# The rotary step of an attention block: pair swaps by a VectorE shuffle instead of swapped projections, and q one slot earlier

## The reference, cut to what matters

```python
x = x + attn(layernorm(x), W_attn, W_proj)       # 16 heads of 8, causal softmax
x = x + ffn(layernorm(x), gate_w, experts)       # 8 experts, Sinkhorn gates, top 64 tokens each

q, k, v = split(x @ W_attn)
q = q * cos + rotate_half(q) * sin               # rotate_half: (x1, x2) -> (-x2, x1) on each pair
k = k * cos + rotate_half(k) * sin
att = softmax(where(causal, q @ k.T / sqrt(8), -inf)); y = att @ v; out = y @ W_proj
```

## Time and profile before

| | us |
|---|---|
| median of 3 runs | 493.18 (491.93 to 494.08) |
| profiled execution, its own time | 492.21 |
| its span, first to last instruction | 490.5 |
| TensorE busy (mean granted clock 0.962 of full) | 418.8 (85%) |
| VectorE busy | 404.0 (82%) |
| ScalarE busy | 308.9 (63%) |
| GpSimd busy | 228.1 (47%) |

### The profile page before, as it was taken

The page is one execution under the profiler, slowest core; times in us unless marked ns, Lnnn a source line. Parts: engine busy times, 40 slices in busy tenths (PEclk is TensorE's granted clock), DMA queues, the critical chain, the costliest instruction groups (busy, mean ns, idle before and its releaser), DMA issues.

```text
span 490.5 us, 9349 instructions
## 1 busy us (share of the span) xinstructions
PE 418.8 (85%) x2827; PEld 209.1 (43%) x2827; DVE 404.0 (82%) x1616; ACT 308.9 (63%) x599; POOL 228.1 (47%) x411
## 2 busy tenths in 40 slices
PE   5448987998999999899999989999988965999563
PEld 4233444464545546344554644555444432434121
DVE  6968756898898789788878978887986876996997
ACT  1002684788678769867876986887777432543871
POOL 3142573567466356746635674543433210000895
PEclk9955988999999999999999999999999999999998
DMA  8770143035027004402701440270001010100122
GB/s 261 213 174 2 49 135 76 34 115 113 21 78 182 25 33 131 99 20 77 182 25 45 126 110 2 97 162 24 2 1 64 2 43 0 43 23 21 43 65 86
DMA packets 28434, 36.85 MB, mean 75 GB/s; under 512 B 2144, under 2 KB 24224, under 8 KB 26912
## 3 DMA queue, kind: packets, MB, share of 16 engines
q1 hardware_dynamic: 27312, 34.68, 25.4%
q10 hardware_dynamic: 1072, 1.57, 1.3%
HBM read 19.41 MB, written 16.78 MB: 74 GB/s over the span
## 4 chain that ended last, share of the span: by engine, by line
PE 53%; DVE 23%; ACT 8%; issue 7%; DMA 5%; POOL 1%; SPq 1%; POOLq 1%; DVEq 1%; ACTq 0%
PE PVB L494 11%; PE ROWB L469 10%; PE CHB L482 9%; PE MB L526 6%; PE MB L502 4%; PE MB L536 4%; ACT YS L736 4%; DVE JUNK L938 3%; DMA YS<-parts_scratch 3%; PE ROWB L628 3%; DVE YS L1229 2%; PE CHB L628 2%; DVE CHB L1229 2%; PE MB L515 2%; DVE X L1235 2%
## 5 line engine op out<-in xcount | busy, mean ns | idle before, releaser
L938 DVE CUSTOM_DVE_ANT_0 JUNK<-ROWB,TRI 128x384 bf16<-128x384 f32 (+3 forms) x512 | 221.7, 485 | 41.7 <-PE ROWB L469 38.2
L736 ACT ACTIVATE YS<-CHB 128x512 f32<-128x512 f32 x320 | 172.9, 612 | 44.0 <-PE CHB L482 43.7
L858 POOL TENSOR_SCALAR_AFFINE_SELECT YS<-YS 128x256 f32<-128x256 f32 x256 | 102.4, 410 | 147.2 <-ACT YS L736 139.4
L469 PE MATMUL ROWB<-YS 96*128 96x384 bf16 (+3 forms) x512 | 122.2, 312 | 13.1 <-DVE MX L938 7.1
L482 PE MATMUL CHB<-YS 104*128 104x384 bf16 (+3 forms) x512 | 116.4, 303 | 7.4 <-ACT YS L736 5.0
L494 PE MATMUL PVB<-YS,VP 128*32 128x512 f32 (+3 forms) x1024 | 95.2, 446 | 5.1 <-POOL YS L858 5.1
L469 PEld LDWEIGHTS ROWB<-YS 96*128 96x128 bf16 x512 | 43.8, 100 | 89.9 <-DVE MX L938 47.1
L696 ACT ACTIVATE YS<-MB 8x1024 bf16<-8x1024 bf16 x32 | 32.5, 1017 | 57.4 <-PE MB L515 57.4
L482 PEld LDWEIGHTS CHB<-YS 104*128 104x128 bf16 x512 | 46.0, 98 | 41.7 <-ACT YS L736 17.6
L494 PEld LDWEIGHTS PVB<-YS,VP 128*32 128x32 f32 x1024 | 35.1, 109 | 31.7 <-POOL YS L858 17.5
L938 DVE DVE_READ_ACCUMULATOR2_ANT MX<- 128x1 f32 x512 | 42.2, 82 | 0.0
(11 more groups left out here) (131 smaller groups left out, 520.0 us busy)
## 6 DMA issues: line engine op xcount, KB each, us to landing
YS<-parts_scratch SPq DMA_DIRECT2D x28, 384.0 KB, 6.7
parts_scratch<-PARTS SPq DMA_DIRECT2D x15, 384.0 KB, 2.4
parts_scratch<-PARTS SPq DMA_DIRECT2D x15, 256.0 KB, 2.1
X<-in_x SPq DMA_DIRECT2D x8, 256.0 KB, 5.4
xn_scratch<-XN2S SPq DMA_DIRECT2D x8, 256.0 KB, 2.0
XS<-xn_scratch SPq DMA_DIRECT2D x8, 256.0 KB, 2.6
out<-X SPq DMA_DIRECT2D x8, 256.0 KB, 2.3
parts_scratch<-PARTS SPq DMA_DIRECT2D x15, 128.0 KB, 1.7
```

The costliest lines, as they stand in the source:

```text
L469: last = pe.matmul(ROWP[BANK[u]][:, col:col + keys], QP[par][0:ROWS_K, pair, P * qb:keys], KZ[par][i % 2][0:ROWS_K, pair, 0:keys], start=T ...
L736: act.activation(PT[s % 2][:, c, :], CH[BANK[c]], ACT.Exp).then_inc(exp_done, 1)
L858: pool.affine_select(out=v, in_=v, pattern=[[0, 2], [1, P]], compare_op=ALU.is_ge, fill=0.0, base=0, channel_multiplier=-1).then_inc(causa ...
L938: last = dve.tensor_tensor_reduce(out=JUNK[BANK[u]][:, col:col + n], in0=ROWP[BANK[u]][:, col:col + n], in1=TRI[:, T - n:T], scale=1.0, sc ...
```

## The change

The swapped projections of the loop leave, and VectorE makes the swap: `stream_shuffle` moves partition i to i ^ 16 within each 32 while it copies from `MB` to `TS`. The product with the sines moves to GpSimd, in front of its sum. `TC` and `TS` exist twice. Projections before the loop (batch 0) still use `WSWAP`. In the plan, q stands at x0 of slot 3 in place of x2, its rotation follows u2 of slot 3 in place of c7, its first part is cut behind c1 of slot 3 and subtracted behind c5; xnT stands at x4 of slot 2 in place of x1 of slot 3; xn2T and the logits go to x1 and x2 of slot 3; the second norm's roots go from slot 1's x3 to slot 2's x0 and its normalisation behind c1 and c6 of slot 2. Six of the eight tiles `OH`, used at the end, now lie over `PARTS`.

```diff
-EXTRAS = {(0, 1): ("k", 1), (0, 2): ("ks", 1), (1, 1): ("yT", -1), (1, 2): ("proj", -1), (1, 3): ("v", 1),
-          (2, 4): ("xn2T", -1), (3, 0): ("logits", -1), (3, 1): ("xnT", 2), (3, 2): ("q", 2), (3, 3): ("qs", 2)}
-ROTATE = {(3, "c", 7): (0, 2), (0, "c", 4): (1, 1)}
-CUT = {(0, "x", 0): (0, 0, 1), (0, "c", 1): (0, 1, 1), (0, "x", 3): (0, 2, 1),
+EXTRAS = {(0, 1): ("k", 1), (1, 1): ("yT", -1), (1, 2): ("proj", -1), (1, 3): ("v", 1),
+          (2, 4): ("xnT", 2), (3, 0): ("q", 2), (3, 1): ("xn2T", -1), (3, 2): ("logits", -1)}
+TURN = [i ^ 16 for i in range(32)]
+ROTATE = {(3, "u", 2): (0, 2), (0, "c", 4): (1, 1)}
+CUT = {(3, "c", 1): (0, 0, 2), (0, "x", 0): (0, 1, 1), (0, "c", 1): (0, 2, 1),
        (1, "x", 0): (1, 0, 1), (1, "v", 1): (1, 1, 1), (1, "c", 1): (1, 2, 1)}
-SUBTRACT = {(0, "u", 2): (0, 0, 1), (0, "c", 1): (0, 1, 1), (1, "u", 2): (1, 0, 1), (1, "u", 3): (1, 1, 1)}
-NORMALIZE = {(2, "u", 1): (0, 3, 2), (2, "c", 7): (3, 4, 2)}
+SUBTRACT = {(3, "c", 5): (0, 0, 2), (0, "u", 2): (0, 1, 1), (1, "u", 2): (1, 0, 1), (1, "u", 3): (1, 1, 1)}
+NORMALIZE = {(2, "u", 1): (0, 3, 2), (2, "c", 4): (3, 4, 2)}
...
-FIRST_EXTRAS = {(0, 1): ("xnT", 1), (0, 2): ("q", 1), (0, 3): ("qs", 1), (0, 4): ("k", 1), (1, 0): ("ks", 1), (1, 3): ("v", 1)}
-FIRST_ROTATE = {(0, "c", 4): (0, 1), (1, "u", 2): (1, 1)}
+FIRST_EXTRAS = {(0, 1): ("xnT", 1), (0, 2): ("q", 1), (0, 3): ("k", 1), (1, 3): ("v", 1)}
+FIRST_ROTATE = {(0, "c", 4): (0, 1), (0, "x", 4): (1, 1)}
...
-RSTD2_AT = (1, "x", 3)
-NORMALIZE2 = {(2, "w", 9): (0, 2), (2, "v", 1): (2, 4)}
+RSTD2_AT = (2, "x", 0)
+NORMALIZE2 = {(2, "c", 1): (0, 2), (2, "c", 6): (2, 4)}
...
             def rotate(w, b):
-                pool.wait_ge(misc_free, BANK_TURN[("qs", "ks")[w], b] + 1)
+                pool.wait_ge(misc_free, BANK_TURN["qk"[w], b] + 1)
+                pool.nop(nofuse=True)
+                pool.tensor_tensor(TS[w][:, :], TS[w][:, :], ROPE[:, 2 * w + 1, :], ALU.mult)
+                pool.drain()
                 if not (isinstance(b, int) and b == 0):
                     pool.wait_ge(part[w], 3 * b)
-                pool.tensor_tensor(RES[w][:, :], TC[:, :], TS[:, :], ALU.add).then_inc(resid[w], 1)
+                pool.tensor_tensor(RES[w][:, :], TC[w][:, :], TS[w][:, :], ALU.add).then_inc(resid[w], 1)
...
-            def turn(b, name, i, w, dst):
-
-                if i % 2 == 0:
-
-                    if w == 1:
-                        dve.wait_ge(resid[0], 3 * b + 1)
-                    elif not (isinstance(b, int) and b == 0):
-                        dve.wait_ge(resid[1], 3 * b - 2)
+            def turn(b, name, w):
+
+                if b > 0:
+                    dve.wait_ge(resid[w], 3 * b - 2)
                 dve.wait_ge(misc_full, BANK_TURN[name, b] + 1)
-                dve.tensor_tensor(dst[:, :], MB[:, :], ROPE[:, i, :], ALU.mult).then_inc(misc_free, 1)
+                dve.tensor_tensor(TC[w][:, :], MB[:, :], ROPE[:, 2 * w, :], ALU.mult)
+                dve.stream_shuffle(TS[w][:, :], MB[:, :], TURN).then_inc(misc_free, 1)
```

More of the change, by code:

```diff
@@ L214, in build @@
         RSTD = sb("RSTD", [P, B * TB])
-        TC = sb("TC", [P, T])
-        TS = sb("TS", [P, T])
+        TC = [sb(f"TC{w}", [P, T]) for w in range(2)]
+        TS = [sb(f"TS{w}", [P, T]) for w in range(2)]
         RES = [sb(f"RES{w}", [P, T]) for w in range(2)]
@@ L248, in build @@
         TOKEN = sb("TOKEN", [P, T], F16)
-        OH = [sb(f"OH{i}", [P, T], BF16) for i in range(8)]
+        OH = [sb(f"OH{i}", [P, T], BF16) for i in range(2)] + [PARTS[w][:, i, :] for w in range(2) for i in range(3)]
         RT = sb("RT", [B * E, T])
@@ L528, in q @@
             def q(b): project(b, "q", WQKV[:, 0:C])
-            def qs(b): project(b, "qs", WSWAP[:, 0:C])
             def k(b): project(b, "k", WQKV[:, C:2 * C])
-            def ks(b): project(b, "ks", WSWAP[:, C:2 * C])
             def by_tiles(b, name, src, weight, n):
@@ L549, in logits @@
             def logits(b): by_tiles(b, "logits", XN2S, WGATE[:, :], E)
-            extras = {"xnT": xn_transposed, "q": q, "qs": qs, "k": k, "ks": ks, "v": v,
+            extras = {"xnT": xn_transposed, "q": q, "k": k, "v": v,
                       "yT": y_transposed, "proj": proj, "xn2T": xn2_transposed, "logits": logits}
@@ L981, in clip_logits @@
                                   MB[:, 0:TB * E], CLIP_EPS, None, ALU.max).then_inc(misc_free, 1)
-            extras = {"q": lambda b: turn(b, "q", 0, 0, TC), "qs": lambda b: turn(b, "qs", 1, 0, TS),
-                      "k": lambda b: turn(b, "k", 2, 1, TC), "ks": lambda b: turn(b, "ks", 3, 1, TS),
+            extras = {"q": lambda b: turn(b, "q", 0), "k": lambda b: turn(b, "k", 1),
                       "proj": add_attention, "logits": clip_logits}
@@ L1009, in first_turn @@
                     dve.wait_ge(resid[0], 1)
-                last = dve.tensor_tensor((TC, TS)[i % 2][:, :], FIRSTB[i], ROPE[:, i, :], ALU.mult)
+                last = dve.tensor_tensor((TC, TS)[i % 2][0][:, :], FIRSTB[i], ROPE[:, i, :], ALU.mult)
                 if i % 2 == 1:
@@ L1015, in first_sum @@
                 dve.wait_ge(first_turned, w + 1)
-                dve.tensor_tensor(RES[w][:, :], TC[:, :], TS[:, :], ALU.add).then_inc(resid[w], 1)
+                dve.tensor_tensor(RES[w][:, :], TC[0][:, :], TS[0][:, :], ALU.add).then_inc(resid[w], 1)
             def first_cut(w, i):
```

## The result

The changed kernel took 487.28 us in the median (485.55 to 488.73, 4 runs) against 493.63 for the kernel before; the ratio is 0.9894, with a 95% interval of 0.9867 to 0.9922: 5.2 us or 1.1% faster. (The two medians lie 6.35 us apart; where this text says 5.2 us it goes by the recorded ratio.) Forecast were 484.0 us and a range of 478.5 to 491.5. The profiled execution took 488.20 us.

A forecast was written before the change was run, and what follows sets the result against it. Bound: TensorE's work, broken by waits at five places. Terms -0.4, -0.55, -0.45 make -1.4 a cycle, -8.4 over six; first slots and last cycle -0.4 each: -9.2, so 484.0 us; own range 480 to 488, 8-in-10 range 478.5 to 491.5.

The forecast's parts named there:

- Slot 3: Cycle term: swapped q leaves, mx waits for the shuffle, ScalarE copies q's first part; -0.4 us, ends -0.96 and 0.
- mx waiting on the shuffle: Slot 3: the turn of the maxima waits 0.4 us until VectorE's product and shuffle free MB.
- 0.96 us of a TensorE without a hole: Slot 3: the swapped q's matmul leaves a TensorE without waits, so its whole 0.96 us is won.
- ScalarE's copy: Slot 3: copying q's first part between exps is 0.5 us of work, of which 0.15 shows at c5.
- k's path: Slot 0 and slot 1 as far as v3: swapped k and waits leave, GpSimd's product delays v3; -0.55 us a cycle.
- The product, put at 1.28: k's rotation on GpSimd, before the clearings of c5 to c7, grows by a product: +1.28 us, ends 1.0 and 1.6.
- Slot 2: Cycle term: GpSimd's root chain no longer holds v3, xn's transposition waits about 0.35; -0.45 us, ends -0.8 and +0.3.
- First slots: First batch: both swapped matmuls leave, GpSimd gets two products in one slot; -0.4 us, ends -2 and +2.
- The last cycle: The last cycle, without q and k, keeps only slot 2's term: -0.4 us.
- Blocked maxima: Rival: GpSimd holds one more minus maxima instruction in each cycle, giving 0.83 us back; 489.0 us, 16 in 100.
- The slow shuffle: Rival: a shuffle of 2.07 us, three passes, holds VectorE, cycle 1.4 us longer; 500.6 us, 9 in 100.
- Given back on GpSimd: Rival: c4's exp comes no earlier, v3 of slot 1 is 1.28 us later; kernel 493 us, 14 in 100.

The follow-up runs named there:

- e1: The changed kernel with the plan of before, so the swap alone without the moves; 497.86 us, ratio 1.0106 to the kernel before.
- e3: The changed kernel without GpSimd's product with the sines in the loop, for q and k; 482.00 us, ratio 0.9786.
- e6: The changed kernel with xn's last tile normalised with the other three, behind u1 of slot 2; 483.75 us, ratio 0.9814.
- e9: e7 with all four normalisations of the second norm behind w9 of slot 3; 477.58 us, ratio 0.9698.
- e4: The changed kernel with k's product moved behind c2 in slot 0, all work done; 483.59 us, ratio 0.9808.
- e8: e7 with batch 0 in the plan of before: k's projection at x4 of slot 0, rotation behind u2 of slot 1; 481.19 us.
- e2: The changed kernel with the second norm's roots and normalisation back at their old places; 492.52 us, ratio 0.9998.
- e7: The changed kernel with e4's early product and e6's early normalisation together; 481.15 us, ratio 0.9760.

## Why the prediction was right in direction and too large in size

The profiled executions differ by 4.0 us. By stretches (starts of v0): first slots of batch 0 +1.3, six cycles -5.6, last cycle -1.2, the end +1.5. Forecast were -0.4, -8.4, -0.4 and 0.

The -5.6 is not six times the steady gain. The steady cycle gained 0.47 us, a third of the 1.4 forecast, and six of those are -2.8. The rest stands in single places: slot 3 of the first cycle (14.31 to 13.42 us, 0.8 more than in a steady one), slot 2 of the last of the six, where xn2's transposition has left and no xn is due (10.51 to 8.94 us, 1.3 more), and the pauses told of below, three before and one after (0.7). The forecast had no term for any of them. That the total came out at over half of the forecast is in part luck. By the forecast's own steps:

- **Slot 3, forecast -0.4, measured -0.11.** The 0.4 for mx waiting on the shuffle was right (0.39). The step that failed is "0.96 us of a TensorE without a hole": e1 shows only 0.30 of it counting, as exps and maxima stood right behind. ScalarE's copy, put at 0.15, can't be read off by itself: the wait of 0.25 before c6 stands in e1 too, which has no copy in slot 3, and slot 3 of the changed kernel is 0.19 longer than e1's with the copy and mx's wait together.
- **k's path, forecast -0.55, measured -0.43 in the cycle of the rows but -0.08 in the others.** The mechanism held in each part: slot 0 got 1.50 (from 11.20) or 1.13 (from 10.83) shorter, and v3 of slot 1 waits 1.01 us for GpSimd, forecast as 0.5 to 1. The product, put at 1.28, was worth 0.77 (e3), and 0.28 of slot 1's excess stays without it. What failed is the base: the wait of 0.33 before the swapped k stood in one cycle of the six, and it is the pause of 0.35 us that the cycle of the earlier trace rows carried in slot 0. I took one cycle and multiplied by six; slot 0 was 10.84 or 10.83 us in the other five.
- **Slot 2, forecast -0.45, measured -0.27.** The wait before v3 is gone, as said. xn's transposition waits 0.66, not 0.35 (e6), and ScalarE's normalisations between exps cost a wait of 0.83 before c5, which I had taken as no worse than before; there the wait was 0.35, in the line below. e9 shows that 0.60 of slot 2 hangs on it.

```profile
246.07 1.37 PE L482 MATMUL CHB<-YS 104*128 104x512 bf16 x5 [0.35 <-ACT YS L736]
```

- **First slots, forecast -0.4, measured +1.3** in the profile (v0 of slot 3 at 75.52 before, 76.80 after), of which u0 of slot 3 feels 0.84 (79.29 to 80.13). One profile of each can't size this term: e4 has the same plan up to there and reaches that v0 at 75.08. e8 shows that the plan of batch 0 isn't what sets its end.
- **The last cycle, forecast -0.4, measured -1.17.** Its slot 2 went from 11.06 us to 10.27 in e2 and to 9.31 in the changed kernel, so xn2's transposition leaving the slot and the roots' move share it; slot 3 gave 0.58 back. I had carried over slot 2's term alone.
- **Blocked maxima**, a rival at 16 in 100, meant one more blocked instruction in each cycle. That did not come: the one in each cycle of before (1.02 us) is gone, in the cycle shown of the changed kernel no such instruction is longer than 0.54 us, and only batch 0 has a new one (1.20). e1 has one a cycle as before, now the second of the two. The second minus maxima instruction, duration ns min/median/max, in e1 and then in the changed kernel:

```profile
L951 DVE SCALAR_TENSOR_TENSOR NMX<-MX,NMX x32: 178/180/1207, 41.6 to 375.9; 128x16 bf16<-128x16 f32 x32
```

```profile
L951 DVE SCALAR_TENSOR_TENSOR NMX<-MX,NMX x32: 178/290/1203, 41.6 to 368.4; 128x16 bf16<-128x16 f32 x32
```

In e1 its mean is 390 ns, in the changed kernel 289, before 236; both instructions together have 653, 609 and 590. The Trainium skill, "SBUF — State Buffer", section "Who interferes with whom", has a VectorE instruction with two SBUF inputs wait for the whole of a GpSimd instruction that reads SBUF; this one has two, and the trace agrees: 1207 ns at the longest, against 1268 ns for GpSimd's sum in e1.

- **The slow shuffle** is ruled out by its row, 729 ns. (The figure that the Trainium skill, "VectorE: DVE Perf Modes", perf-mode tier table, has for 2048 elements gave an estimate of 0.6 to 0.7 us for 512; the trace has slightly more, and the mask load beside it is 14 ns.) **Given back on GpSimd** is what e1 is: with the plan of before the 1.05 us lost in slot 1 (by e3, 0.77 of it the product's) outweigh the 0.30 and 0.22 won in slots 3 and 0.
- **The forecast's own range of 480 to 488** doesn't follow from its terms: half the way to the ends of each, added up, is -2.6 to +0.1 us a cycle in place of -1.4, and so about 476 to 494 us with the first slots.

The median's change (-5.2 by the ratio) is larger than the profile's; two of the four runs of the changed kernel, the profiled one among them, had a mean clock of 0.947 to 0.949 and took 488.2 and 488.7 us, the two at 0.959 and 0.962 took 486.4 and 485.6. The steady cycle alone doesn't give the medians either: e2's is 0.30 us above that of before and its median the same, so the single places named above count in every kernel with q's move.

## What to carry to other kernels

Before counting a removed matmul in full, look at what stands directly behind it in its engine's order and how much slack that has: 0.96 us of a fully busy TensorE was worth 0.30 (e1, slot 3). Work moved to an idle engine costs by its place in that engine's order, not by its length: the same 1.28 us product costs 0.77 us in front of three clearings and 0.22 us two steps earlier, where the engine was idle. And read a loop over all its rounds before multiplying one of them: one round carried a pause, and the first and the last ones changed by other amounts than the steady ones.

## What the runs showed of the hardware

TensorE's granted clock fell to its lower level (1.2 GHz) near 395 us in the changed kernel, behind the loop, where the kernel before stayed at the upper one. Windows of TensorE alone, changed kernel and then the kernel before:

```profile
390.00:395.00 5.00, 3.21 (x18) 0.93 0.31 102
395.00:400.00 5.00, 5.00 (x10) 0.50 0.01 5
400.00:405.00 5.00, 4.05 (x9) 0.50 0.00 0
```

```profile
395.00:400.00 5.00, 3.34 (x18) 1.00 0.30 95
400.00:405.00 5.00, 3.29 (x10) 1.00 0.03 12
```

Both have 18 instructions in one window and 10 in the next, with TensorE busy for 3.2 and 3.3 of 5 us in the first, once with the fall and once without. The price can be read from the same pair of matmuls in the changed kernel and then in the kernel before:

```profile
395.38 2.02 PE L627 MATMUL CHB<-WEXP,XS 128*128 128x512 f32 x2
```

```profile
400.40 1.08 PE L628 MATMUL CHB<-WEXP,XS 128*128 128x512 f32 x2
```

Of the +1.5 us of the end 1.16 lies there, in a part that the change hardly touches: at 391.03 the changed kernel is 5.23 us ahead of the kernel before, at 414.39 it is 4.07 ahead, at the same instructions. The fall is no mark of the change. Every experiment's profile has one there, of different length: e7 and e8, which differ in batch 0 alone, had granted clocks of 0.77, 0.50, 0.71 and of 0.66 in windows of 5 us, and ends of 119.3 and 118.7 us. The kernel before had mean clocks from 0.946 to 0.962 over all its runs. Why it falls in one run and not in another stays open.

The kernel before also shows pauses of about 0.35 us in three of its steady cycles, each in another slot (10.65 in place of 10.29, 10.79 in place of 10.51, 11.20 in place of 10.83); the changed kernel shows one (9.99 in place of 9.70). TensorE's waits in them name VectorE or GpSimd: 0.43 in place of 0.18 us before u3, 0.92 in place of 0.64 before v3, and the 0.33 before the swapped k. What held those engines there I did not find, and the cause is open.
